# Selective-scan block with a ternary FFN: the softplus stage and the FFN's high parts on other engines

## What is computed

```python
xx, res = split(x @ in_w.T)                       # 512 inner channels each
u = silu(causal_conv(xx, 4 taps) + conv_b)
dt, B, C = split(u @ xproj_w.T)                   # 16, 16, 16
delta = softplus(dt @ dt_w.T + dt_b)              # [512 channels, 512 steps]
h_t = exp(delta * A) * h_{t-1} + delta * B * u    # 16 states for each channel
y = sum_n(C_n * h_n) + u * D
x = layernorm(x + (y * silu(res)) @ out_w.T)
h = silu(s1 * (x @ w1.T)) * (s2 * (x @ w2.T))     # 1024 hidden, ternary weights
h = gelu(t1 * (h @ h1.T)); h = gelu(t2 * (h @ h2.T))
x = layernorm(x + s3 * (h @ w3.T))
```

## Time and profile before

| what | us |
|---|---|
| median of 3 runs (lowest, highest) | 3149.71 (3144.48, 3151.66) |
| the profiled execution's own time | 3155.72 |
| its span, first to last instruction | 3153.9 |
| busy: PE, DVE, ACT, POOL | 2583.1 (82%), 2621.1 (83%), 2343.3 (74%), 1071.0 (34%) |

### The profile page before, as it was taken

The page is one execution under the profiler, slowest core; times in us unless marked ns, Lnnn a source line. Parts: engine busy times, 40 slices in busy tenths (PEclk is TensorE's granted clock), DMA queues, the critical chain, the costliest instruction groups (busy, mean ns, idle before and its releaser), DMA issues.

```text
span 3153.9 us, 41504 instructions
## 1 busy us (share of the span) xinstructions
PE 2583.1 (82%) x12290; PEld 1944.8 (62%) x12290; DVE 2621.1 (83%) x2625; ACT 2343.3 (74%) x3653; POOL 1071.0 (34%) x1028
## 2 busy tenths in 40 slices
PE   4355788888888888988888898888888889898888
PEld 1223566676666666676666766666676756666666
DVE  3678998989898897989889898988989898998830
ACT  2776687877969787796968779697877969687822
POOL 0112333333433433343343334234333423423432
PEclk8566899999989999999989999899999989899999
DMA  1996787787878778787887878787787878778933
GB/s 52 290 321 140 167 193 180 185 197 184 194 179 193 190 181 186 183 194 183 190 188 179 194 181 194 179 196 189 178 190 181 200 186 196 189 180 191 229 111 110
DMA packets 230192, 585.49 MB, mean 186 GB/s; under 512 B 26016, under 2 KB 26400, under 8 KB 229808
## 3 DMA queue, kind: packets, MB, share of 16 engines
q0 software_dynamic: 73728, 268.47, 46.2%
q1 hardware_dynamic: 119344, 246.86, 22.4%
q10 hardware_dynamic: 36864, 67.13, 7.9%
HBM read 281.93 MB, written 31.98 MB: 100 GB/s over the span
## 4 chain that ended last, share of the span: by engine, by line
PE 32%; DVE 29%; ACT 17%; issue 14%; DMA 4%; ACTq 1%; DVEq 1%; SPq 1%; POOL 1%; POOLq 0%
PE ffn_ps L479 17%; DVE scan_ps L782 11%; DVE hC L792 5%; PE scan_ps L367 5%; ACT dB L616 4%; ACT dA L607 3%; DVE y L806 3%; PE misc_ps L372 3%; DMA x<-ffn_w 3%; PE misc_ps L423 2%; DVE gate L899 2%; PE misc_ps L460 2%; PE misc_ps L408 2%; ACT L607 2%; PE misc_ps L367 2%
## 5 line engine op out<-in xcount | busy, mean ns | idle before, releaser
L782 DVE TENSOR_TENSOR_SCAN scan_ps<-dA,scan_ps 128x1024 f32<-128x1024 f32 x512 | 1170.8, 2287 | 57.0 <-PE scan_ps L367 33.2
L968 POOL DMA_DIRECT2D y<-hC x512 | 446.1, 871 | 1811.2 <-DVE hC L792 1735.1
L367 PE MATMUL scan_ps<-ident,dB 128*128 128x128 f32 x4096 | 613.4, 300 | 375.7 <-DVE hC L792 292.3
L367 PEld LDWEIGHTS scan_ps<-ident,dB 128*128 128x128 f32 x4096 | 519.9, 154 | 521.2 <-DVE hC L792 305.5
L616 ACT ACTIVATE dB<-duT,bT 128x512 f32<-128x512 f32 x1024 | 726.4, 711 | 154.5 <-PE scan_ps L367 153.2
L607 ACT ACTIVATE dA<-delta,a_neg 128x512 f32<-128x512 f32 (+1 forms) x1024 | 710.1, 712 | 41.1 <-DVE hC L792 38.0
L479 PE MATMUL ffn_ps<-hb_hi,ring 128*128 128x512 f32 x1536 | 660.1, 430 | 18.4 <-DVE gate L899 8.7
L792 DVE TENSOR_TENSOR hC<-scan_ps,c_rows_sb 128x1024 f32<-128x1024 f32 x512 | 623.6, 1218 | 49.8 <-DMA y<-hC 41.5
L479 PE MATMUL ffn_ps<-hb_lo,ring 128*128 128x512 f32 x1536 | 620.7, 404 | 0.0
L479 PE MATMUL ffn_ps<-ha_hi,ring 128*128 128x512 f32 x1024 | 443.5, 433 | 2.4 <-POOL ha_lo L990 2.4
L479 PE MATMUL ffn_ps<-ha_lo,ring 128*128 128x512 f32 x1024 | 407.7, 398 | 0.0
(11 more groups left out here) (90 smaller groups left out, 2941.9 us busy)
## 6 DMA issues: line engine op xcount, KB each, us to landing
y<-hC POOLq DMA_DIRECT2D x512, 512.0 KB, 5.8
ring<-split_weights SPq DMA_DIRECT2D x704, 256.0 KB, 4.3
c_rows_sb<-c_rows ACTq DMA_DIRECT2D x256, 256.0 KB, 4.0
xt<-x_tok SPq DMA_DIRECT2D x32, 512.0 KB, 6.1
x<-ffn_w SPq DMA_DIRECT2D x22, 512.0 KB, 9.7
split_weights<-ha_hi SPq DMA_DIRECT2D x22, 512.0 KB, 5.2
split_weights<-ha_lo SPq DMA_DIRECT2D x22, 512.0 KB, 7.0
out_tok<-out_st SPq DMA_DIRECT2D x16, 512.0 KB, 2.9
```

The source lines that it names most:

```text
L367: mm = nc.tensor.transpose(dst[:, j * P:(j + 1) * P], src(j), ident[:])
L782: nc.vector.tensor_tensor_scan(b, dA[:, a:a + 2, :].rearrange("p a l -> p (a l)"), b, 0.0, ALU.mult, ALU.add).then_inc(scan_done, 1)
L968: pool.dma_start(y2[:, par, c:c + 2, :], hC[:, p % 2], accum_op=ALU.add).then_inc(y_added[p % 2], 16)
```

## The change

What it does, in four parts:

- PSUM plus bias (L818) goes from DVE to ACT: in the slot after PE's dt tile ACT reads `misc_ps` twice, as |v + b| into `du` and as max(v + b, 0) into `delta2`; the second gives `dt_ready`. ACT's exp(-|v|) of tile 3 moves from slot 48 to slot 45 with it. DVE's w and lost bits move one slot up (43, 44, 45, 48).
- max(v,0) - lost (L837), the sum with ln (L843), du (L848) and y = D u (L854) go from DVE to POOL as `tensor_tensor`, in slots 44, 45, 46, 49; 52, 52, 53, 53; 53, 53, 54, 54; and 57 to 60. For y = D u the scalar is read as a tile with a stride of zero.
- The FFN's hi copies (L697, L710) go from ACT to POOL: `split_tile` on POOL makes the copy and then the subtraction, in the slot in which ACT made the copy (`HI_AT`), so the subtraction's slot is one earlier than before.
- On POOL the new `front_step` is called last in a slot, behind `y_pair`, gate and FFN.

```diff
-A_HI, A_LO = 2, 3
+A_LO = 2
-LO_AFTER = 1
+LO_AFTER = 0
-F_DT, F_EXP, F_PLUS, F_MAX, F_LN = (41, 42, 43, 44), (43, 44, 45, 48), (44, 45, 46, 49), (45, 46, 47, 50), 51
-F_DELTA, F_DELTA_U, F_Y, F_DU = (54, 54, 55, 55), (54, 54, 55, 55), (57, 58, 59, 60), (56, 57, 58, 59)
+F_DT, F_PLUS, F_SUB, F_LN = (41, 42, 43, 44), (43, 44, 45, 48), (44, 45, 46, 49), 51
+F_DELTA, F_DELTA_U, F_Y, F_DU = (52, 52, 53, 53), (53, 53, 54, 54), (57, 58, 59, 60), (56, 57, 58, 59)
@@ ACT, front_step
-                for c in range(DC):
-                    if F_EXP[c] != s:
-                        continue
-                    act.wait_ge(dt_ready, r * DC + (c + 1))
-                    nc.scalar.activation(du[:, c, :], delta2[:, par, c, :], ACT.Abs).then_inc(sp_abs, 1)
+                if s - 1 in F_DT:
+                    c = F_DT.index(s - 1)
+                    act.wait_ge(pe_dt, r * DC + (c + 1))
+                    nc.scalar.activation(du[:, c, :], misc_ps[:], ACT.Abs, bias=ch[:, c, C_DTB:C_DTB + 1]
+                                         ).then_inc(sp_abs, 1)
+                    nc.scalar.activation(delta2[:, par, c, :], misc_ps[:], ACT.Relu, bias=ch[:, c, C_DTB:C_DTB + 1]
+                                         ).then_inc(dt_ready, 1)
@@ POOL, new
+            def front_step(r, par, s):
+                for c in range(DC):
+                    if F_SUB[c] == s:
+                        pool.wait_ge(dt_ready, r * DC + (c + 1))
+                        pool.wait_ge(sp_lost, r * DC + (c + 1))
+                        nc.gpsimd.tensor_tensor(delta2[:, par, c, :], delta2[:, par, c, :], du[:, c, :], ALU.subtract
+                                                ).then_inc(sp_base, 1)
+                for c in range(DC):
+                    if F_DELTA[c] == s:
+                        pool.wait_ge(sp_base, r * DC + (c + 1))
+                        pool.wait_ge(sp_ln, r * DC + (c + 1))
+                        nc.gpsimd.tensor_tensor(delta2[:, par, c, :], delta2[:, par, c, :], sp_w[c], ALU.add
+                                                ).then_inc(delta_ready, 1)
+                for c in range(DC):
+                    if F_DELTA_U[c] == s:
+                        pool.wait_ge(u_ready, r * DC + (c + 1))
+                        pool.wait_ge(delta_ready, r * DC + (c + 1))
+                        nc.gpsimd.tensor_tensor(du[:, c, :], y2[:, par, c, :], delta2[:, par, c, :], ALU.mult
+                                                ).then_inc(du_ready, 1)
...
-            def low_tile(f, i):
+            def split_tile(f, i):
+
+                if i < HC:
+                    pool.wait_ge(l1_x32, f * HC + (i + 1))
+                else:
+                    if i == 2 * HC:
+                        pool.wait_ge(pe_half, f * HALVES + 2 * HC)
+                    pool.wait_ge(gelu_x32, f * (2 * HC) + (i - HC + 1))
+                hi, lo = (hb_hi, hb_lo) if HC <= i < 2 * HC else (ha_hi, ha_lo)
+                pool.sem_inc(split_begun, 1)
+                nc.gpsimd.tensor_copy(hi[:, i % HC, :], x32[:, i % X32, :]).then_inc(ffn_hi, 1)
                 pool.wait_ge(ffn_hi, f * FFN_TILES + (i + 1))
                 nc.gpsimd.tensor_tensor(lo[:, i % HC, :], x32[:, i % X32, :], hi[:, i % HC, :].bitcast(F32),
                                         ALU.subtract).then_inc(ffn_lo, 1)
```

More of the change, by code:

```diff
@@ L212, in build @@
         gelu_x32, ffn_hi, ffn_lo = sem("gelu_x32"), sem("ffn_hi"), sem("ffn_lo")
+        split_begun = sem("split_begun")
         w3_scaled, z2_ready, out_ready = sem("w3_scaled"), sem("z2_ready"), sem("out_ready")
@@ L689, in gelu_tiles @@
                                          scale=fs[:, 2 + i // HC, i % HC:i % HC + 1]).then_inc(gelu_x32, 1)
[L691 to L697, removed]
             def ffn_step(f, s):
@@ L832, in front_step @@
                                                    op0=ALU.subtract, op1=ALU.subtract).then_inc(sp_lost, 1)
-                for c in range(DC):
-                    if F_MAX[c] != s:
-                        continue
-                    dve.wait_ge(sp_lost, r * DC + (c + 1))
-                    nc.vector.scalar_tensor_tensor(out=delta2[:, par, c, :], in0=delta2[:, par, c, :], scalar=0.0,
-                                                   in1=du[:, c, :], op0=ALU.max, op1=ALU.subtract).then_inc(sp_max, 1)
-                for c in range(DC):
-                    if F_DELTA[c] == s:
-                        dve.wait_ge(sp_max, r * DC + (c + 1))
-                        dve.wait_ge(sp_ln, r * DC + (c + 1))
-                        nc.vector.tensor_tensor(delta2[:, par, c, :], delta2[:, par, c, :], sp_w[c], ALU.add
-                                                ).then_inc(delta_ready, 1)
-                for c in range(DC):
-                    if F_DELTA_U[c] == s:
-                        dve.wait_ge(delta_ready, r * DC + (c + 1))
-                        nc.vector.tensor_tensor(du[:, c, :], y2[:, par, c, :], delta2[:, par, c, :], ALU.mult
-                                                ).then_inc(du_ready, 1)
-                for c in range(DC):
-                    if F_Y[c] != s:
-                        continue
-                    dve.wait_ge(du_ready, r * DC + (c + 1))
-                    nc.vector.tensor_scalar(y2[:, par, c, :], y2[:, par, c, :], ch[:, c, C_D:C_D + 1], None,
-                                            ALU.mult).then_inc(y_init, 1)
             def statistics(which, src, r, half, ready):
@@ L968, in y_pair @@
                 pool.dma_start(y2[:, par, c:c + 2, :], hC[:, p % 2], accum_op=ALU.add).then_inc(y_added[p % 2], 16)
+            def front_step(r, par, s):
[17 more added lines that the diff above has]
+                                                ).then_inc(du_ready, 1)
+                for c in range(DC):
+                    if F_Y[c] == s:
+                        pool.wait_ge(pe_dbl, r + 1)
+                        pool.wait_ge(du_ready, r * DC + (c + 1))
+                        nc.gpsimd.tensor_tensor(y2[:, par, c, :], y2[:, par, c, :],
+                                                ch[:, c, C_D:C_D + 1].to_broadcast([P, SEQ]), ALU.mult
+                                                ).then_inc(y_init, 1)
             def gate_tile(r, par, c):
@@ L1013, in iteration @@
                         ffn_step(end, s + TILES)
+                    if front is not None:
+                        front_step(front, fpar, s)
             iteration(-1, 1)
```

18 lines of the change are left out of this document (3 added, 15 removed).

## The result

The changed kernel takes 3162.78 us, the median of 7 runs (3161.40 to 3166.59); the kernel before took 3149.71 in its 7 runs beside them (3144.48 to 3155.80). The ratio is 1.0044, with a 95% interval of 1.0032 to 1.0055: **slower by 13 us**, where 45 were forecast. The profiled execution took 3163.39 us (span 3161.6).

What follows compares the result with a forecast made beforehand. PE was taken to be bound by the dates of the last du and last lo tile, both set by POOL; 1.1 + 1.7 + 0.4 = 3.2 us in 14 iterations, 45 us, gives 3195 by the median; range 3143 to 3262.

Steps and rivals of the forecast that it cites:

- What bounds the kernel: Whole iteration: two dates decide it, last du ready (slot 56) and last lo tile ready (slot 11), both set by POOL.
- The date of du: POOL's chain from slot 49's y DMA: 20.1 us without rest, last du at 1549.0 instead of 1547.93, 1.1 us later.
- much slower: Rival: copy at 1.6, L831 waiting 1.1 us, half clock lasting 6.7 us; 9.5 us by 14, 3283 us; chance 0.11.
- The clock at du: Behind the wait for du: half clock moves onto back-to-back half tiles, 3.3 us of it losing 1.7 us.
- The last layer: Slot 9: two splits on POOL end 1.95 us later, PE's next transposes 0.4 us later; the wait behind was ACT's.
- ACT's relief: 24 copies go, four PSUM reads come: net 11.8 us a sequence, nearly all beside a busy PE.
- The reads of dt on ACT: Before slot 46: reads end 0.3 to 1 us before PE asks; cost nothing, 0.5 us a sequence without that cover.
- The y DMA behind du: Slot 55: issued at 1549.0, lands 5.8 us later, when slot 59's product wants it; nothing extra in the middle case.
- The ends: Iteration -1 costs +4.8 us on POOL, iteration 0 relieves DVE about as much; sum zero, give or take 5.
- faster: Rival: POOL's chain (16 us, not 20.1) ends before PE is ready; 4.2 us by 14, 3091 us; chance 0.15.

## Why the forecast was right in its sign and wrong in its size

For one iteration, by stages of PE's own queue (each from one transposes of dB to another), means over twelve iterations of both traces. What the half clock costs is PE's busy time multiplied by one minus the granted clock:

| stage | forecast | measured: length | of it PE idle | of it half clock |
|---|---|---|---|---|
| slots 48 to 61, with the wait for du | +2.8 (1.1 wait, 1.7 clock) | +2.9 | +0.9 | +2.3 |
| slots 62 to 7 | 0 | -0.4 | -0.2 | -0.3 |
| slots 8 to 13, the last layer | +0.4 | -1.5 | -0.5 | -0.8 |
| slots 14 to 47 | 0 | -0.1 | -0.2 | +0.1 |
| sum | +3.2 | +0.9 | 0.0 | +1.2 |

(Idle time and half clock are counted separately from the length and give it to within 0.2 us a stage, 0.4 in the sum.)

**What bounds the kernel: right for the changed kernel.** POOL's lo tile and du are what PE waits for in it. The run with du alone on VectorE shows that the date of du decides there, and the last two copies on ACT that the last layer does. Without the chain on POOL it is not du alone (the last column above). But "DVE is busy for 16.07 of 16.10 us" was read as work. It held 2.1 us of being locked out by POOL's subtractions, and the forecast had the rows to see it: it used them (0.67 to 1.78 us) for a rival only, not as something that the kernel before already paid and a moved subtraction could give back.

**The date of du: right for the wrong reasons.** At the eighth sequence du was forecast at 1549.0, which is 165.8 us after the first scan, and ended at 1551.61, 165.9 after it. Two errors cancel. The copy was taken at 0.9 us and takes 0.60, and a two-input operation is a step of 1.24, not 1.28, so the chain from the start of slot 49's y DMA to the last du was 19.5 us long, not 21.0. And it started 1.6 us late. 0.5 of that stood already at the scan; the rest is VectorE's step ahead of the product, which the forecast had put at 0.69 from the earlier trace rows and kept the longer price for the "much slower" case. VectorE's timeline:

```profile
1525.86 2.30 DVE L771 TENSOR_TENSOR_SCAN scan_ps<-dA,scan_ps 128x1024 f32<-128x1024 f32 x1 [1.58 <-PE scan_ps L368]
1528.06 0.55 DVE L813 TENSOR_SCALAR out_st<-du 128x512 f32<-128x512 f32 x1
1528.64 1.66 DVE L815 SCALAR_TENSOR_TENSOR du<-out_st,du 128x512 f32<-128x512 f32 x1
```

A subtraction on POOL ran beside it from 1528.41. That was no rare mishap: it is so in 13 of 16 sequences, and this form of L815 takes 1096 ns in the mean and w = 1 + e for the gate tiles 1107, against 692 and 417 before. With 2.3 us more on w for the other tiles this is 37 of the 72 us by which DVE's relief fell short of the count. The rest is overlap: added up one by one DVE's operations shrank by 212 us, but neighbours overlap, and the busy time, which counts each moment once, by 174.5. The term itself came out smaller, 0.4 us in the mean instead of 1.1, because the iteration chosen was a favourable one for the kernel before (du transposes at 164.8 against 165.2 in the mean), though 14 were called alike.

**The clock at du: the mechanism right, a third too small.** The half clock does fall on the half tiles behind the wait, over 6.83 us in the eighth sequence instead of the 3.3 taken, and costs 2.2 us in the mean. But it was not moved there: the stretch around slot 54 costs as much as before (2.1 and 2.0 us), and in the kernel before it did not fall "mostly into waiting", since PE worked for 3.82 of its 6.70 us. That PE would stand ready at 1545 was right in size only: it did at 1547.14, which is 1544.6 by the earlier rows, but the wait that went was the 2.34 us for the product, and that for ACT's dB, which was to shrink by 1.8, stayed (3.94 and 3.84), since PE came to it earlier by as much as dB did.

**The last layer: the step that failed.** It was to cost 0.4 us and gave 1.5 back: 1.9 us by 14, or 27 of the 32 us of error. The stage at du with its clock came out at 2.9 us for 2.8. The forecast said that the 1.52 us wait there was caused by ACT "which is relieved of two copies", so that the wait would go; yet it booked only POOL's delay, and put at nothing the stretch at half clock behind it, which costs 0.8 us in the mean. Both went, and putting the two copies back brought 21 us. The copy's price of 0.60 is the second half of the same step: with it the two splits take 0.6 us less than forecast. The 0.4 us in slots 62 to 7 were not forecast either, and their cause stays open.

**ACT's relief: a large miss, hidden by the sum.** 11.8 us a sequence were called worth nearly nothing, save 1.8 us of a wait. With the delta stage on VectorE, moving the copies off ACT is worth 3.9 an iteration, of which 2.1 are the lockout above; with it on POOL it takes away POOL's 3.0 us wait for ln, without which the change would have cost 47 us.

**The reads of dt on ACT: right, nothing.** PE has no idle time in slots 42 to 47 in the twelve iterations of either trace. **The y DMA behind du:** VectorE's product of slot 57 waits 5.87 us for the DMA of slot 53, which stands between sums in POOL's chain. PE does not wait for it here: it is busy without a gap from 1551.67 to 1564.49. **The ends: inside the margin, not by their terms.** The first iteration cost 6.3 to 7.2 us, not 4.8 (4.9 of it are the sum and du; for the rest, max - lost on POOL is the likely cause, not tested), and 4.3 came back behind the last scan, where the FFN has ACT without its copies; the kernel with the copies alone moved gains the same there (148.1 us instead of 152.5). **The rivals:** "faster" needed a POOL chain of 16 us, and it was 19.5; with the sum and du left on VectorE the time lies below its 3091.

## What to carry to other kernels

Before work is moved off an engine that looks full, look for its operations that are longer than their own shortest: what they wait for inside may go without moving them (three copies moved elsewhere gave 27 us). Put on the slow engine what has slack (copies, max - lost, y = D u) and keep the chain that others wait for on the engine with the cheaper link: eight links at 1.24 us instead of 0.60 turned a gain of 74 us into a loss of 13. And where a wait is said to go, book what stands behind it too, its stretch of half clock above all.

## What the runs showed of the hardware that was not expected

- A copy from fp32 to fp32r of 128x512 on POOL takes 0.60 us (0.68 from start to start), half of a subtraction of the same shape (1.24 to 1.28), and not the 0.9 that was taken for a fixed part. The Trainium skill's GPSIMD Engine Reference (Engine selection) had it at roughly line rate, and the trace agrees.
- The lockout between DVE and POOL also hits a DVE operation with one SBUF input and a scalar: w = 1 + e for the gate tiles takes 417 ns in the kernel before and 1107 in the mean, up to 1.99 us, in the changed one, where POOL's max - lost runs beside it (in the eighth sequence from 1518.23 to 1519.80, w from 1518.10 to 1520.09). With the copies alone moved it stays at 0.42.
- Two operations on POOL that nobody waits for cost 28.7 us over the program.
- In the last layer, 0.4 us more of idle time of PE (2.1 instead of 1.7) went with 3.4 us at 1.2 GHz that were absent without it. Over the kernels, 2.1 to 2.2 us of idle time there go with 0.5 to 0.8 us lost to the clock, and 1.7 with 0 to 0.3.
